# Decoder layer on one core: FFN weights made in units inside the attention slots, the last two heads' output projection by batch

## The reference, cut to what matters

```
x = x + attention(layernorm(x))        # causal, rope, q/k/v/o weights = (codes - 8) * scales
x = x + fake_quant(layernorm(x)) @ fake_quant(ctx)      # 8-bit grids, zero point 128
x = x + layernorm(x) @ bw.T            # the FFN
bw = mean(|w|, axis=1) * sign(w) - clip(w, -1, 1) + clip(w, -1, 1)
```

## Time and profile before

| | |
|---|---|
| median of 3 runs | 1196.02 us |
| the profiled execution | 1195.91 us |
| its span, first to last instruction | 1194.1 us |
| PE, DVE, ACT, POOL busy | 94%, 77%, 55%, 49% |
| stage 2, 64 slots | 219.3 to 987.7 us |
| stage 3 up to the first cross attention | 987.7 to 1061.5 us |
| the loop over 8 token tiles | 1061.5 to 1194.1 us |

### The profile page before, as it was taken

One profiled execution on the slowest core, in us unless ns is written; L12 is line 12 of the kernel. 1 busy time (PEld: TensorE's weight loads), 2 busy tenths in 40 slices (PEclk: granted clock), 3 DMA queues, 4 the chain that ended last, 5 costly groups with the idle time before them and its releaser, 6 DMA issues.

```text
span 1194.1 us, 19855 instructions
## 1 busy us (share of the span) xinstructions
PE 1119.3 (94%) x5988; PEld 566.2 (47%) x5988; DVE 914.8 (77%) x1458; ACT 651.2 (55%) x1414; POOL 581.8 (49%) x644
## 2 busy tenths in 40 slices
PE   3799999899999999999999999999999998379998
PEld 2344444345545455554545455555555543355553
DVE  6867531368888888888888888888888878978773
ACT  2444321466677777777777766566565554533220
POOL 0122000477677676767667676767676654320000
PEclk9999999999999999999999999999999999679999
DMA  7343331256686766666666756655555655210111
GB/s 252 104 141 107 124 105 28 49 126 144 128 163 141 155 146 157 151 147 161 137 163 138 162 131 131 136 130 134 126 138 121 110 96 152 90 69 19 36 36 53
DMA packets 258972, 144.32 MB, mean 121 GB/s; under 512 B 210145, under 2 KB 218593, under 8 KB 258913
## 3 DMA queue, kind: packets, MB, share of 16 engines
q1 hardware_dynamic: 253584, 134.53, 47.4%
q10 hardware_dynamic: 5328, 9.05, 3.0%
HBM read 89.00 MB, written 4.19 MB: 78 GB/s over the span
## 4 chain that ended last, share of the span: by engine, by line
PE 86%; DVE 6%; DMA 2%; ACT 1%; issue 1%; SPq 1%; POOL 1%; DVEq 0%; POOLq 0%; ACTq 0%
PE side_ps L472 9%; PE side_ps L473 9%; PE side_ps L474 9%; PE side_ps L583 9%; PE out_ps L604 9%; PE proj_ps L604 8%; PE proj_ps L472 6%; PE proj_ps L474 6%; PE proj_ps L473 6%; PE score_ps L566 3%; PE score_ps L569 3%; PE score_ps L570 3%; PE score_ps L698 2%; PE score_ps L567 1%; DVE x_acc L1303 1%
## 5 line engine op out<-in xcount | busy, mean ns | idle before, releaser
L1053 POOL TENSOR_TENSOR w_b<-prob,w_b 128x896 f16<-128x896 f32 (+2 forms) x192 | 188.2, 994 | 46.0 <-ACT w_b L888 45.9
L472 PE MATMUL side_ps<-hT,w_a 128*128 128x512 f16 x512 | 194.5, 380 | 6.8 <-DVE rot L1248 6.8
L1303 DVE SCALAR_TENSOR_TENSOR x_acc<-proj_ps,o_now,x_acc 128x1024 f32<-128x1024 f32 x124 | 158.3, 1277 | 51.3 <-PE proj_ps L604 51.2
L1041 POOL TENSOR_TENSOR swapped<-swapped,sin_t 128x512 f32<-128x512 f32 x80 | 101.9, 1274 | 193.2 <-ACT swapped L800 193.1
L473 PE MATMUL side_ps<-hT,w_a 128*128 128x512 f16 x512 | 194.5, 380 | 0.0
L474 PE MATMUL side_ps<-hT,w_a 128*128 128x512 f16 x512 | 194.3, 379 | 0.0
L1046 POOL TENSOR_SCALAR prob<-prob,row_inv 128x512 f32<-128x512 f32 (+3 forms) x256 | 164.0, 654 | 16.1 <-DVE row_inv L1337 11.9
L858 ACT ACTIVATE prob<-score_ps,neg_max 128x512 f32<-128x512 f32 (+3 forms) x256 | 132.2, 519 | 55.7 <-POOL w_b L1053 45.5
L1060 POOL TENSOR_TENSOR q_sb<-rot,q_sb 128x512 f16<-128x512 f32 x64 | 74.1, 1158 | 178.2 <-ACT q_sb L850 178.2
L1303 DVE SCALAR_TENSOR_TENSOR x_acc<-out_ps,o_now,x_acc 128x1024 f32<-128x1024 f32 x124 | 157.7, 1271 | 0.0
L604 PE MATMUL proj_ps<-work,w_b 128*128 128x512 f16 x512 | 131.4, 379 | 2.9 <-DVE x_acc L1303 2.8
(11 more groups left out here) (187 smaller groups left out, 2116.4 us busy)
## 6 DMA issues: line engine op xcount, KB each, us to landing
stage_c<-in_codes_dram SPq DMA_DIRECT2D x96, 256.0 KB, 2.7
stage_s<-in_scales_dram SPq DMA_DIRECT2D x96, 256.0 KB, 3.7
stage_o<-in_codes_dram SPq DMA_DIRECT2D x64, 256.0 KB, 3.7
ctx_raw<-in_ctx_dram ACTq DMA_DIRECT2D x32, 256.0 KB, 3.4
x_acc<-in_x_dram SPq DMA_DIRECT2D x8, 512.0 KB, 9.6
work<-w_b SPq DMA_TRANSPOSE x256, 3.0
hT<-in_ffn_w_dram SPq DMA_DIRECT2D x8, 512.0 KB, 4.1
w_b<-in_x_dram SPq DMA_DIRECT2D x8, 512.0 KB, 3.3
```

The costliest lines, as they stand in the source:

```text
L472: pe.matmul(o, stat(0), mov(0), start=first, stop=False)
L1041: pool.tensor_tensor(swapped[:, :], swapped[:, :], sin_t[:, :], ALU.mult).then_inc(done, 1)
L1053: ins = pool.tensor_tensor(prob16[:, 1, to:to + w], prob[:, at:at + w], prob16[:, 0, to:to + w], ALU.subtract)
L1303: ins = dve.scalar_tensor_tensor(y, u, s, y, ALU.mult, ALU.add)
```

## The change

It has four parts.

**(a) Rings.** `o_codes` and the Q weights keep 2 heads and not 4. That frees the second half of w_a (for 2 of the FFN's 8 row blocks of bw, in both halves) and of w_b's first row (work space of the units).

**(b) The FFN's weights in 32 units of 128 x 256.** The means come first: in the V stage ACT issues 16 loads of 128 x 512 and takes |w| / 1024 with its sum of each (`abs_part`, tiles 13 to 29). Unit u is then made in the slots: for u = 0 to 7 around slots 0 to 7, for u = 8 to 31 from slot 40 on, when K's and V's groups 4, 5 and 6 are read for the last time. In the slot of `wf_early`: POOL clips, ACT takes the sign, DVE the difference, POOL adds. In the slot of `wf_late`: ACT makes the high half, DVE the rest, and SP issues two DMA transposes (`turn_wf`) into the second half of w_a or K's and V's free groups. The 64 transposes on PE, their PSUM reads and the work on 128 x 1024 behind the slots are gone. Unit 0 is made ahead of slot 0, and DVE's `wf_difference(0)` stands ahead of DVE's slot 0.

**(c) The last two heads by batch.** `two_units` makes 256 output rows of one batch, and `add_two` adds them in two instructions. Head 30 is made in slots 62 and 63, where no Q projection is left, head 31 batch 0 behind slot 63; x1 of batch 0 (`turn_y` 0 to 3) comes ahead of the last `weigh`, then head 31 batch 1 and x1 of batch 1. The column sums of the context are spread between them.

**(d) Smaller things.** x goes whole into hT's space, so its loads wait for nothing. Groups 5 to 7 are written out and not looped.

```diff
+RING = 2
+WF_PAIRS = KB // 2
+WF_UNITS = WF_PAIRS * KB
+WF_FROM = (NKV - WF_PAIRS + 1) * SLOTS
+ABS_FROM = KV_TILES - 2 - 2 * KB
...
 def each_group(eng, body):
             with eng.Fori(1, CTX_GROUPS + 1) as g:
                 body(g, True)
-            with eng.Fori(CTX_GROUPS + 1, NKV - 1) as g:
+            for g in range(CTX_GROUPS + 1, NKV):
                 body(g)
-            body(NKV - 1)
...
+            def turn_wf(u):
+                q, t = divmod(u, KB)
+                for l, done in ((0, wf_hi), (1, wf_split)):
+                    sp.wait_ge(done, u + 1)
+                    sp.dma_start_transpose(bw_pair(q, l)[:, :, t * P:(t + 1) * P], wf_halves[:, l, :])\
+                        .then_inc(wf_turned, 16)
...
             def body(g, with_ctx=False):                      # SP
                 for i in range(SLOTS):
+                    p = g * SLOTS + i
                     next_pieces(g, i)
+                    if known(p):
+                        if p == 0:
+                            sp.wait_ge(proj_done, KV_TILES)
+                        for u in wf_loads(p):
+                            load_wf(u)
+                        if wf_late(p) is not None:
+                            turn_wf(wf_late(p))
...
+                    turn(p)
...
+                if known(p) and p == N_SLOTS - 2:             # PE
+                    scores(p, i, g, 0)
+                    o_unit(p - 1, prev[1], 3)
+                    scores(p, i, g, 1)
+                    o_unit(p, i, 0)
+                    scores(p, i, g, 2)
+                    for k in range(1, UNITS):
+                        o_unit(p, i, k)
+                    for k in range(UNITS):
+                        two_units(NH - 2, 0, k)
+                    weigh(p - 1, prev[1], prev[0])
+                    return
+                if known(p) and p == N_SLOTS - 1:
+                    for u in range(3):
+                        scores(p, i, g, u)
+                        two_units(NH - 2, 1, u)
+                    two_units(NH - 2, 1, 3)
+                    column_sums(0, 0)
+                    weigh(p - 1, prev[1], prev[0])
+                    return
...
+            column_sums(0, 1)                                 # PE, behind the slots
+            column_sums(1, 0)
+            for k in range(UNITS):
+                two_units(NH - 1, 0, k)
+            for t in range(TB):
+                turn_y(t)
             weigh(N_SLOTS - 1, SLOTS - 1, NKV - 1)
+            column_sums(1, 1)
+            for k in range(UNITS):
+                two_units(NH - 1, 1, k)
+            for t in range(TB, TT):
+                turn_y(t)
             turn_i1(0)
             cross(0)
...
                 exps(p, i, 1)                                 # ACT
+                if known(p) and wf_late(p) is not None:
+                    wf_upper(wf_late(p))
...
                 if has_ahead:
                     q_swap(p + Q_AHEAD)
+                if known(p) and wf_early(p) is not None:
+                    wf_sign(wf_early(p))
                 if has_prev:
                     ao_part(p - 1, (i - 1) % SLOTS)
...
                     norm(2).then_inc(norm_done, 1)            # POOL
+                    if known(p) and wf_early(p) is not None:
+                        wf_clip(wf_early(p))
...
                     prob_rest(p, 1)
+                    if known(p) and wf_early(p) is not None:
+                        wf_add(wf_early(p))
...
+                if known(p) and wf_late(p) is not None:       # DVE, behind 1 / sum
+                    wf_lower(wf_late(p))
                 if has_piece:
                     piece_lo(n, i % 2, q_region(i), Q_UP)
...
                 if has_ahead:
                     q_cos(p + Q_AHEAD)
+                if known(p) and wf_early(p) is not None:
+                    wf_difference(wf_early(p))
                 if has_prev:
                     ao_rest(p - 1, (i - 1) % SLOTS)
...
+            wf_lower(WF_UNITS - 1)                            # DVE, behind the slots
+            add_two(NH - 1, 0, 0)
+            column_part(0, 1)
+            add_two(NH - 1, 0, 1)
+            column_part(1, 0)
+            add_two(NH - 1, 0, 2)
+            add_two(NH - 1, 0, 3)
             x1_part(0)
             x1_part(1)
             x1_stats(0, 0)
             row_roots(2, x1_stats(1, 1))
+            dve.wait_ge(prob_lo[1], N_SLOTS)
             x1_norm(0, 0)
+            x1_part(2)
             x1_norm(1, 1)
+            x1_part(3)
+            ao_rest(N_SLOTS - 1, SLOTS - 1)
+            column_part(1, 1)
             x1_quant(0)
+            add_two(NH - 1, 1, 0)
             x1_quant(1)
+            for k in range(1, UNITS):
+                add_two(NH - 1, 1, k)
+            for t in range(TB, TT):
+                x1_part(t)
```

More of the change, by code:

```diff
@@ L454, in _ @@
-            load_xs(2)
-            load_wf(5)
-            load_xs(3)
-            load_wf(6)
-            load_xs(4)
-            load_wf(7)
-            for t in range(5, TT):
+            turn_wf(WF_UNITS - 1)
+            for t in range(2, TT):
                 load_xs(t)
@@ L634, in slot, with two_units @@
                     weigh(p - 1, prev[1], prev[0])
-            def column_sums(b):
-                if b == 0:
+            def two_units(h, b, k):
+                n = TWO_FROM + ((h - NH + 2) * B + b) * UNITS + k
+                if k % 2 == 0:
+                    pe.wait_ge(o_codes_done, N_SLOTS - (NH - 1 - h) * B - (1 - k // 2))
+                if k == 0:
+                    pe.wait_ge(ao_ready, h * B + b + 1)
+                if (h, b) == (NH - 1, B - 1) and k < 2:
+                    pe.wait_ge(x1_ready, k + 3)
+                else:
+                    pe.wait_ge(o_added, n - 1)
+                for x in range(2):
+                    for l in range(2):
+                        mm = pe.matmul(o_banks[n % 2][:, x, :], o_codes[:, h % RING, (2 * k + x) * P:(2 * k + x + 1) * P],
+                                       ao[:, h % 2, l, b * S:(b + 1) * S], start=l == 0, stop=l == 1)
+                mm.then_inc(o_done, 1)
@@ L639, in column_sums @@
+            def column_sums(b, h):
+                if (b, h) == (0, 0):
                     pe.wait_ge(scal_ready, 1)
                     pe.wait_ge(ctx_free, 2 * B * KB + 1)
[L641 to L648 removed]
@@ L666, in turn_y @@
+                for k in range(KB):
+                    mm = pe.matmul(col_ps(b, h), ones_b[:, :], i2_tile(b * KB + k)[:, h * S:(h + 1) * S],
+                                   start=(k == 0), stop=(k == KB - 1))
+                mm.then_inc(col_summed, 1)
             def turn_y(t):
-                if t == 0:
-                    pe.wait_ge(o_added, N_UNITS)
+                pe.wait_ge(o_added, N_UNITS - UNITS if t < TB else N_UNITS)
                 if t >= 2:
@@ L715, in dense @@
             def dense(t):
+                if t == 0:
+                    pe.wait_ge(wf_turned, 2 * 16 * WF_UNITS)
                 for h in range(NB):
@@ L1304, in o_add, with add_two @@
                 ins.then_inc(o_added, 1)
+            def add_two(h, b, k):
+                dve.wait_ge(o_done, TWO_FROM + ((h - NH + 2) * B + b) * UNITS + k + 1)
+                u = o_banks[k % 2]
+                for x in range(2):
+                    y, cb = x_acc[:, 2 * k + x, b * S:(b + 1) * S], 2 * k + x
+                    ins = dve.scalar_tensor_tensor(y, u[:, x, :], o_now[:, h % 2, cb:cb + 1], y, ALU.mult, ALU.add)
+                ins.then_inc(o_added, 1)
             def ao_rest(p, i):
```

379 lines of the change are left out of this document (171 added, 208 removed).

## The result

The changed kernel takes 1189.95 us (median, 1188.64 to 1190.47), the kernel before on the same chip 1196.38; the ratio is 0.9942, 95% interval 0.9925 to 0.996. That is 6.4 us faster, where 18 were forecast. The profiled execution has a span of 1188.0 us against 1194.1.

What follows compares the result with a forecast made beforehand. PE was taken to bound the slots, DVE the stretch from slot 62 to cross(0). Span 1194.1 + 0 + 3.5 + 1 - 22.5 = 1176.1 us, forecast time 1178; range 1171 to 1186.

Steps and rivals of the forecast that it cites:

- The tail's size: From slot 62 to cross(0), DVE sets the pace; cross(0) comes 22.5 us earlier, bounds -17 and -27.
- DVE, difference: gap 0.45 us. 0.41 fits, with nothing to spare: In the unit slots, ahead of L1310: DVE's 0.41 us difference fits a gap of 0.45 us.
- DVE, rest [...] It fits: In the unit slots, ahead of L1157: DVE's 0.41 us rest fits where DVE waits 0.56 us for ACT.
- +1 for the slots: Unit work in the slots' gaps: 30 x 0.03 = +1 us, bounds 0 and +3.3.
- rival A: Slots pay 0.11 us each, as context slots do, and the clock is low through cross(0): 1183.7 us; chance 0.20.
- The bound from the context slots: Upper bound for a unit's slot, from slots with more ACT work: 0.9% or 0.11 us of 12.1.
- Writing groups 5 and 6 out costs nothing: Slot code written out, not looped: no cost, as group 7 was written out before with PE busy throughout.
- The start: Slots 0 to 3: unit 0 delays slot 0 by 2.1 us, clips add 1.4; +3.5, bounds +1.5 and +5.
- The V stage: 16 loads and 16 absolute sums on ACT while PE works without a gap: 0, up to +1 us.
- rival D: Units' DMA transposes hold SP or its queue longer than the rows show; at 3.6 us a call 1226 us; chance 0.04.
- C: At the end, a later weigh(61) holds back slot 62's transposes, so slot 63 waits: +10, 1188 us; chance 0.08.
- E: Units run late in every slot, so the FFN's dense(0) waits for the last transposes; chance 0.01.

## Why the prediction was right or wrong

- **The tail's size was right, -22.1 measured for -22.5, in part by luck.** With the 17.6 us that the slots had lost by weigh(60), my places read `weigh(61)` 1001.8, cross(0) 1056.6; the trace has 1002.08 and 1057.04. DVE does set the pace there, so its hand-made order, with durations from the earlier trace rows, gave the first half. Behind it two errors cancel. `weigh(62)` came 2 us later than said (1015.80 for 1013.6), with the clock at 0.66 from 1010 to 1015 us, and the last four `turn_y` began 3.4 us later (1050.78 for 1047.4). But from there to cross(0) it took 6.3 us and not 9.2: I had put these four at the low clock, as in the earlier trace rows, and they ran at 1.00 (matmuls 0.11 us apart). By my own sum the full clock alone was worth 2.7 us more, so the order of DVE that I made by hand was about 3 us too short.
- **"DVE, difference: gap 0.45 us. 0.41 fits, with nothing to spare" failed, and "DVE, rest [...] It fits" with it.** The term was +1 for the slots with a bound of 3.3, and 6.1 was measured. First, the 0.41 was read from a row whose instruction has an operand in PSUM (L1373); the two new steps have both operands in SBUF, and free of POOL they take 0.47 and 0.43. Second, they are not free of POOL. The rest lasts 0.78, makes POOL's norm beside it take 1.26 instead of 0.58, and so sends the sine back by 0.6 us; the sine then stands across the difference, which lasts 0.94; and behind both the copy of the scales lasts 0.62. The row that I held against myself in rival A, DVE's L1157 with 0.96 us beside a busy POOL, was this very effect (the 20 of its 80 instances with no POOL beside them take 0.69): I priced the new steps by their group's mean and did not ask what POOL runs at that moment. The clip fits into ACT's wait, as said, and moves the sine by 0.08 us. The bound from the context slots, 0.11 us a slot, was no bound: what counts is which instructions meet, not how many there are.
- **"Writing groups 5 and 6 out costs nothing" was right for them, and the question was too narrow.** The loop of groups 1 to 4 lost 4.5 us by its place in ACT's stream. (From weigh(2) to weigh(40) it is +4.2: slots 4 to 8 add 0.7, the loop's other slots give 1.0 back.) The prediction had no term for it, and no row of before could have shown more than that its jumps cost nothing.
- **The start was short by half**, 6.6 for 3.5; other executions with the same start lie at +4.9 to +6.8, so a part of that is chance. Slot 0's mechanism was right: the first Q matmul at 225.51 for 225.0 forecast. Missing were the clock, three stretches at half instead of one, and slots 1 and 3, where the difference runs into the sine as in the late slots (1.10 and 1.22 us).
- **The V stage** cost nothing, as said: from 63 us to the first score PE has no gap above 0.2 us in either trace. **SP's transposes**, the slower-side rival D, cost nothing: a pair is issued in 2.4 us (1.17 and 1.25), as calls of the rows, not by blocks. A, C and E did not happen: A's price for the slots, 3.3 us, was about half of the 6.1, and its low clock through cross(0) did not come.
- So three terms of one sign (+5.1 in the late slots, +3.1 and 0.7 of jitter at the start, +4.2 in the loop), less 1.7 at the end, and -22.1 for -22.5, make the 12 us between 1178 and 1190. The range's upper end came from the tail's clock and 2.3 us of the slots. It left out the bound that the earlier trace rows gave: a DVE step held for a whole POOL instruction, an estimated 0.5 us in half or all of 30 slots, 8 to 15 us.

## What to carry to other kernels

When a step is laid into a gap, write down what the engine that shares its memory side runs in that gap after everything has moved, and price the step by waiting for that whole instruction; a step that is hidden on its own engine can still make the neighbour late, and so push it under the next one. Look at a loop's distance across its jump back after any change ahead of it, even when its body is the same, and move it with work in idle places if it has begun to fetch. Work that fills spare time is worth ordering by the free places of each engine: the same steps, with the jumps among them, cost 14.6 us by ratio in one order and 4.9 in another.

## What the hardware showed that was not expected

- An empty instruction (a wait already met) costs ACT 0.2 us: 64 moved its table load from 3.50 to 16.70 us.
- A loop of 291 instructions on ACT (331 in the profile) costs 1.5 us a jump at 384 to 675 of its stream as built and nothing at 314, 322 or 448; 5 packets of 8 KB on the instruction queue go with each turn.
- A copy of 128x8 words on DVE takes 0.15, 0.39 or 0.62 us by when it is issued against POOL's running instruction; 0.1 us decides.
- POOL's norm of 128x384 takes 0.58 us, and 1.26 us where a DVE instruction with both operands in SBUF went ahead of it.
- At waits of PE of 1.60 to 3.87 us the granted clock fell to half (1.2 GHz), mostly for some 3 us, but the length of the wait did not tell whether: the same first wait of 3.87 us was followed by it in the changed kernel and not in the one with 64 empty instructions at the head, and the wait of 1.97 us was followed by it in the version with unit 0 moved and not in the kernel before. With 12 matmuls into a free bank within each wait it stayed at 2.4 GHz, in both versions that have them.
